# Attention stacks of block 0: two split parts per transfer by way of a buffer in memory, mask rows from memory, clearing moved to GpSimd

## The reference, cut to what matters

```
for i in range(NL):                                       # NL = 6 layers
    ...                                                   # self attention
    q = rope((xn @ cq_w[i].T).reshape(B, L, H, HD))       # 16 sequences x 56 queries
    k = rope((context @ ck_w[i].T).reshape(B, LC, H, HD)) # 16 sequences x 1500 keys
    v = (context @ cv_w[i].T).reshape(B, LC, H, HD)       # H = 16 heads of HD = 8 features
    scores = einsum('bqhd,bkhd->bhqk', q, k) / sqrt(HD)
    scores = where(mask, -inf, scores)
    x = x + einsum('bhqk,bkhd->bqhd', softmax(scores), v).reshape(B, L, D) @ co_w[i].T
    ...                                                   # MLP
```

## Time and profile before

| | us |
|---|---|
| median of 3 runs | 7625.0 |
| the profiled execution's own time | 7628.34 |
| its span, first to last instruction | 7626.5 |
| first and last query transfer issued in block 0 | 236.2 and 4312.5 |
| mean granted TensorE clock, share of full | 0.891 |

### The profile page before, as it was taken

How to read it: one execution, slowest core, us unless ns; L and a number is a source line. 1 busy time by engine, 2 the same in 40 slices (tenths; PEclk the granted TensorE clock), 3 DMA queues, 4 the chain that set the end, 5 groups by cost and what they waited for, 6 DMA issues and landing times.

```text
span 7626.5 us, 148949 instructions
## 1 busy us (share of the span) xinstructions
PE 6404.8 (84%) x58485; PEld 4540.6 (60%) x58485; DVE 4073.1 (53%) x8998; ACT 3384.9 (44%) x6385; POOL 2280.8 (30%) x2182
## 2 busy tenths in 40 slices
PE   5587877878787887878786788999987999999998
PEld 3365555546465555546464436777764777774883
DVE  2465666656565666656565452444444444445562
ACT  1355554555454554545454432344432333332573
POOL 4344444434443444434443200000000111107440
PEclk6698988989898888889888897999987999999997
DMA  1455445555555545554454301000000000003000
GB/s 42 70 78 79 80 78 84 76 82 79 81 77 80 81 78 82 79 83 77 81 78 78 51 29 22 33 33 29 29 20 20 13 13 13 13 9 101 1 1 20
DMA packets 405818, 410.92 MB, mean 54 GB/s; under 512 B 134791, under 2 KB 382162, under 8 KB 403074
## 3 DMA queue, kind: packets, MB, share of 16 engines
q1 hardware_dynamic: 405122, 401.39, 30.6%
HBM read 158.00 MB, written 0.46 MB: 21 GB/s over the span
## 4 chain that ended last, share of the span: by engine, by line
PE 43%; SPq 33%; issue 7%; POOL 5%; DVE 4%; ACT 4%; DMA 3%; POOLq 1%; DVEq 0%; ACTq 0%
SPq L1443 17%; PE psum L2251 9%; PE psum L2218 8%; SPq L1452 8%; SPq L1464 7%; PE psum L2263 3%; PE psum L1587 3%; PE psum L1532 3%; POOL slot_context L3407 2%; DMA query_stack<-query_parts 2%; PE psum L437 2%; PE psum L1565 2%; PE psum L423 2%; PE psum L1552 2%; POOL key_parts L2078 1%
## 5 line engine op out<-in xcount | busy, mean ns | idle before, releaser
L1928 DVE TENSOR_REDUCE row_max<-psum 128x1 f32<-128x500 f32 x2304 | 1449.2, 670 | 842.0 <-PE psum L1552 838.2
L2048 ACT ACTIVATE weights<-psum 125x448 f32<-125x448 f32 x2304 | 1230.6, 543 | 1452.3 <-PE psum L1532 1439.9
L1532 PEld LDWEIGHTS psum<-query_stack,key_stack 128*125 128x125 bf16 x9216 | 795.1, 146 | 624.3 <-issue 453.2
L1532 PE MATMUL psum<-query_stack,key_stack 128*125 128x112 bf16 x9216 | 1031.4, 238 | 121.6 <-ACT weights L2048 121.1
L1552 PE MATMUL psum<-key_stack,query_stack 64*64 64x500 bf16 x4608 | 502.5, 425 | 676.9 <-DMA query_stack<-query_parts 527.3
L2775 POOL TENSOR_TENSOR l_ctx_v<-l_ctx_v,l_ctx_w 125x512 f32<-125x512 f32 x48 | 61.0, 1271 | 2286.1 <-DVE l_ctx_v L2769 2286.1
L2251 PE MATMUL psum<-l_ctx_v,l_turned 125*128 125x128 f32 x5376 | 713.6, 281 | 16.4 <-ACT l_turned L2289 12.4
L1565 PE MATMUL psum<-weights,values 125*17 125x112 f32 x18432 | 719.9, 278 | 0.7 <-issue 0.5
L2331 DVE TENSOR_REDUCE l_stat<-psum 128x1 f32<-128x1500 f32 (+1 forms) x224 | 391.6, 1748 | 574.3 <-PE psum L2218 574.3
L2251 PEld LDWEIGHTS psum<-l_ctx_v,l_turned 125*128 125x128 f32 x5376 | 643.1, 191 | 59.2 <-ACT l_turned L2289 40.2
L2075 POOL TENSOR_TENSOR key_temp<-key_temp,key_parts 128x500 f32<-128x500 f32 x288 | 327.2, 1136 | 1054.8 <-ACT key_parts L1954 1054.8
(11 more groups left out here) (531 smaller groups left out, 10514.9 us busy)
## 6 DMA issues: line engine op xcount, KB each, us to landing
key_stack<-key_parts SPq DMA_DIRECT2D x3456, 62.5 KB
ctx_t<-in_ctxT SPq DMA_DIRECT2D x96, 750.0 KB
l_ctx_v<-in_ctxV SPq DMA_DIRECT2D x32, 750.0 KB
key_stack<-ctx_mask_rows SPq DMA_DIRECT2D x1152, 3.9 KB
query_stack<-query_parts SPq DMA_DIRECT2D x1152, 14.0 KB
l_ctx_t<-in_ctxT SPq DMA_DIRECT2D x16, 750.0 KB
slot_context<-in_ctxV SPq DMA_DIRECT2D x16, 750.0 KB
sm_w<-in_sm_w SPq DMA_DIRECT2D x3, 2048.0 KB
```

The source lines that it names most:

```text
L1532: mm = e.matmul(self.k.psum[0:KN, h, (p % 4) * QC:(p % 4 + 1) * QC], ks[:, p, kt * KN:(kt + 1) * KN], q[:, p * QC:(p + 1) * QC])
L1928: e.tensor_reduce(self.largest[:, TWOS * h + p // 2, c:c + 1], k.psum[:, 2 + h, 0:500], AX.X, ALU.max, negate=True).then_inc(self.max_read ...
L2048: e.activation(half(self.p[kt % 2], h), self.k.psum[0:KN, h, 0:HALF], ACT.Exp).then_inc(self.exped.sem, 1)
```

## The change

All of it is in block 0, save for three semaphores that are now shared with a late block under new names.

- A chunk of keys is first written from `key_parts` to a DRAM buffer in one DMA (`write_keys`, [128, 3, 500], four buffers). SP waits for it to land, then issues 6 DMAs from DRAM into the stack instead of 12 from SBUF. Each carries two parts of 64 features, that is 16 partitions and 128 pieces of 1000 bytes. Its source is [2 parts, 64 features, 500 columns], with the part first. In one of three the same part is read twice, with a step of 0.
- Part order in the stack changes from keys 0,0,1,1,0,2 with queries 0,1,0,1,2,0 to keys 0,1,0,0,1,2 with queries 0,1,1,2,0,0: the same six products.
- Queries likewise: one write to DRAM, a wait, 6 DMAs of 16 partitions.
- The mask is written to DRAM once; per slot 2 DMAs of 8 pieces of 3000 bytes replace 12.
- `key_parts` and `query_parts` are free again when the write has landed, not when the stack is filled.
- SP's order in a slot becomes: stack chunk 0 with masks, write chunk 1, weights, write and stack queries, stack chunk 1, write chunk 2, fetch, stack chunk 2, write the next slot's chunk 0.
- The clearing in the loop goes from DVE to POOL at the same step, with a drain before, between and after its two copies.

```diff
-K_PARTS, Q_PARTS = (0, 0, 1, 1, 0, 2), (0, 1, 0, 1, 2, 0)
-PART_ROW = (0, 8, 16, 24, 48, 56)
+K_PARTS, Q_PARTS = ((0, 1), (0, 0), (1, 1)), ((0, 1), (1, 1), (0, 0))
+PART_ROW = (0, 16, 48)
...
+def two_parts(a, h, first, step):
+    v = a[64 * h:64 * h + 64, first:first + 1 + step, :]
+    return (v if step else v.broadcast_to([64, 2, a.shape[2]])).rearrange("q i c -> i q c")
...
+        self.k_memory = k.nc.dram_tensor("key_parts_memory", (4, 128, 3, 500), BF16).ap()
+        self.mask_memory = k.nc.dram_tensor("ctx_mask_memory", (B, L), BF16).ap()
+        self.q_memory = k.nc.dram_tensor("query_parts_memory", (128, 3, QC), BF16).ap()
...
+    def write_keys(self, e, s, c):
+        n = 3 * s + c
+        e.wait_ge(self.key_lo.sem, self.key_lo(s, c))
+        e.dma_start(self.k_memory[n % 4], self.k_part[n % 2][:, :, :]).then_inc(self.part_written[n % 2].sem, 16)
+
     def stack_keys(self, e, s, c):
-        part, sem = self.k_part[n % 2], self.part_stacked[n % 2].sem
+        part, sem = self.k_memory[n % 4], self.part_stacked[n % 2].sem
-        e.wait_ge(self.key_lo.sem, self.key_lo(s, c))
+        e.wait_ge(self.part_written[n % 2].sem, self.part_written[n % 2](n // 2))
+        if n >= 2:
+            e.wait_ge(sem, self.part_stacked[n % 2](n // 2 - 1))
-        for i, j in enumerate(K_PARTS):
+        for row, two in zip(PART_ROW, K_PARTS):
             for h in range(2):
-                row = 64 * h + PART_ROW[i]
-                e.dma_start(dst[row:row + F1, :, c * 500:(c + 1) * 500], part[64 * h:64 * h + 64, j, :]).then_inc(sem, 16)
+                lo = 64 * h + row
+                e.dma_start(dst[lo:lo + 2 * F1, :, c * 500:(c + 1) * 500], two_parts(part, h, *two)).then_inc(sem, 16)
...
-            for n in range(6):
-                for row in (32, 96):
-                    e.dma_start(dst[row:row + 1, :, n * 250:(n + 1) * 250],
+            for row in (32, 96):
+                e.dma_start(dst[row:row + 1, :, :], self.mask_memory[b:b + 1, :].unsqueeze(1).broadcast_to(
+                    [1, PAIRS, L])).then_inc(self.mask_stacked.sem, 16)
+
+    def write_queries(self, e, s):
+        e.wait_ge(self.q_lo.sem, self.q_lo(s))
+        if s >= 1:
+            e.wait_ge(self.q_stacked[(s - 1) % 3].sem, self.q_stacked[(s - 1) % 3]((s - 1) // 3))
+        e.dma_start(self.q_memory, self.q_part[:, :, :]).then_inc(self.q_written.sem, 16)
...
@@ def gpsimd
+                if kt == 7 and 3 <= s + 2 < NS:
+                    e.drain()
+                    self.clear(e, s + 2)
+                    e.drain()
                 self.key_gpsimd(e, s, kt)
```

More of the change, by code:

```diff
@@ L1295, in __init__ @@
         self.ctx_arrived = [ev(f"ctx_t{i}_arrived", NS // 2, step=16) for i in range(2)]
-        self.part_stacked = [ev(f"key_part{i}_stacked", NS * 3 // 2, step=32 * len(K_PARTS)) for i in range(2)]
-        self.mask_stacked = ev("key_mask_stacked", NS, step=192)
-        self.q_stacked = [ev(f"query_stack{i}_arrived", NS // 3, step=32 * len(Q_PARTS)) for i in range(3)]
+        self.part_stacked = [ev(f"key_part{i}_stacked", NS * 3 // 2, step=32 * len(PART_ROW)) for i in range(2)]
+        self.mask_stacked = ev("key_mask_stacked", NS, step=32, base=16)
+        self.q_stacked = [ev(f"query_stack{i}_arrived", NS // 3, step=32 * len(PART_ROW)) for i in range(3)]
         self.key_turned = ev("l0_key_turned", NS, 3)
@@ L1317, in __init__ @@
         self.cleared = ev("l0_max_cleared", NS)
+        self.part_written = [ev(n, NS * 3 // 2, step=16) for n in ("key_part0_written_or_slot_w", "key_part1_written_or_consts")]
+        self.q_written = ev("query_parts_written_or_sigma", NS, step=16)
+        self.k_memory = k.nc.dram_tensor("key_parts_memory", (4, 128, 3, 500), BF16).ap()
+        self.mask_memory = k.nc.dram_tensor("ctx_mask_memory", (B, L), BF16).ap()
+        self.q_memory = k.nc.dram_tensor("query_parts_memory", (128, 3, QC), BF16).ap()
         self.scored = ev("l0_scored", NS, KT, 2)
@@ L1446, in stack_keys @@
                 e.wait_ge(self.masks_ready.sem, self.masks_ready())
+                e.dma_start(self.mask_memory.rearrange("b (n c) -> (b n) c", n=6), self.mask_rows).then_inc(
+                    self.mask_stacked.sem, 16)
+                e.wait_ge(self.mask_stacked.sem, self.mask_stacked(0) - 32)
             else:
@@ L1449, in stack_keys @@
             b = s % B
-            for n in range(6):
-                for row in (32, 96):
-                    e.dma_start(dst[row:row + 1, :, n * 250:(n + 1) * 250],
-                                self.mask_rows[6 * b + n:6 * b + n + 1, :].unsqueeze(1).broadcast_to(
-                                    [1, PAIRS, 250])).then_inc(self.mask_stacked.sem, 16)
+            for row in (32, 96):
[6 more added lines that the diff above has]
+        e.dma_start(self.q_memory, self.q_part[:, :, :]).then_inc(self.q_written.sem, 16)
     def stack_queries(self, e, s):
         dst, sem = self.q_stack[s % 3], self.q_stacked[s % 3].sem
-        e.wait_ge(self.q_lo.sem, self.q_lo(s))
+        e.wait_ge(self.q_written.sem, self.q_written(s))
         if s >= 3:
             e.wait_ge(self.scored.sem, self.scored(s - 3, KT - 1, 1))
-        for i, part in enumerate(Q_PARTS):
+        for row, two in zip(PART_ROW, Q_PARTS):
             for h in range(2):
-                row = 64 * h + PART_ROW[i]
-                e.dma_start(dst[row:row + F1, 0:QW].rearrange("j (p c) -> j p c", p=PAIRS),
-                            self.q_part[64 * h:64 * h + 64, part, :]).then_inc(sem, 16)
+                lo = 64 * h + row
+                e.dma_start(dst[lo:lo + 2 * F1, 0:QW].rearrange("j (p c) -> j p c", p=PAIRS),
+                            two_parts(self.q_memory, h, *two)).then_inc(sem, 16)
     def fetch(self, e, s):
@@ L1500, in sync @@
             if 0 <= s + 2 < NS:
+                if s + 2 == 0:
+                    self.write_keys(e, 0, 0)
                 self.stack_keys(e, s + 2, 0)
-            if 0 <= s + 2 < NS:
-                self.stack_keys(e, s + 2, 1)
+                self.write_keys(e, s + 2, 1)
             if s >= 0 and b == 7 and l + 1 < NL:
@@ L1517, in sync @@
             if 0 <= s + 2 < NS:
+                self.write_queries(e, s + 2)
                 self.stack_queries(e, s + 2)
-                self.stack_keys(e, s + 2, 2)
+                self.stack_keys(e, s + 2, 1)
+                self.write_keys(e, s + 2, 2)
             if 2 <= s + 4 < NS:
                 self.fetch(e, s + 4)
+            if 0 <= s + 2 < NS:
+                self.stack_keys(e, s + 2, 2)
+            if 1 <= s + 3 < NS:
+                self.write_keys(e, s + 3, 0)
     def score_tensor(self, e, s, kt, h):
@@ L1803, in others, with clear @@
             "r (g c x) -> r g c x", g=TWOS, c=2)[:, :, :, h * S:(h + 1) * S]
-    def clear_vector(self, e, b):
+    def clear(self, e, b):
         if b >= 3:
@@ L1809, in clear_vector @@
         for h in range(2):
+            if h == 1:
+                e.drain()
             op = e.tensor_copy(self.others(b, h, 16), self.no_max[64 * h + 32:64 * h + 48, :].unsqueeze(2).unsqueeze(
@@ L1909, in vector @@
         for b in range(3):
-            self.clear_vector(e, b)
+            self.clear(e, b)
         e.drain().then_inc(self.ones_ready.sem, 1)
@@ L1930, in vector @@
                 self.fixed_vector(e, s, kt)
-                if kt == 7 and 3 <= s + 2 < NS:
-                    self.clear_vector(e, s + 2)
         e.wait_ge(self.side.emptied("down", 2 * NL), self.side.after("down", 2 * NL))
@@ L1962, in fixed_scalar @@
             if b > 0:
[L1963 removed]
+                e.wait_ge(self.q_written.sem, self.q_written(b - 1))
             e.activation(self.q_part[:, 0, :], self.q_tmp[:, 0, :], ACT.Copy).then_inc(self.q_hi.sem, 1)
@@ L2975, in __init__ @@
         self.z1, self.around, self.z2 = (spent[:, i * G:(i + 1) * G] for i in range(3))
-        self.raw_arrived = sig("slot_w_arrived", step=48)
+        self.raw_arrived = sig("key_part0_written_or_slot_w", step=48)
         self.ctx_arrived = [sig(f"ctx_{'tv'[i // 2]}{i % 2}_arrived", 4, step=16) for i in range(4)]
         self.ctx_ready = sig("ctx_normed", B)
-        self.made = sig("consts_ready")
-        self.sigma_ready = sig("slot_sigma_ready")
+        self.made = sig("key_part1_written_or_consts")
+        self.sigma_ready = sig("query_parts_written_or_sigma")
         self.folded = sig("heads_folded", 2)
```

3 lines of the change are left out of this document (1 added, 2 removed).

## The result

The changed kernel takes 10,040.85 us (median of 4 runs, 10,038.11 to 10,043.6) against 7630.98 (now 4 runs): a ratio of 1.3163, with a 95% interval of 1.3138 to 1.3189. The forecast was 10,330, the range 8800 to 12,300.

What follows compares the result with a forecast made beforehand. SP's issuing was nearly full, with key transfers a second limit. After the change two engines carry 63.4 us of work plus 7.5 of waits, 70.9 a slot for 42.8; over 96 slots 2698, plus 5, on 7628: 10,330 us, range 8800 to 12,300.

Steps and rivals of the forecast that it cites:

- Engine count: Block 0 stack transfers: the source leads with 2 parts, so they run on 2 engines, the same 2 each time.
- Price of a key piece: Block 0 key stack transfers: 45 ns for each 1000-byte piece from memory, 51.8 us a slot on the two engines.
- Queries: Block 0 query stack transfers: 384 pieces of 224 bytes at 17 ns, 6.5 us a slot.
- Waits for the added writes: SP in block 0 waits for its writes to land while the two engines run dry: 7.5 us a slot.
- the rest: Other block 0 work on the two engines: fetch 1.8 us, key writes 2.8, query write and masks 0.5 a slot.
- A miss without effect: SP's own writes in block 0 were to land 15 us and more after issue, queued behind six transfers.
- Clearing at nothing: Clearing moved from DVE to POOL in block 0 costs nothing; without cover, 2.3 us a slot, 220 us.
- Computation never starves the queue: Block 0 computation needs 37 us a slot and goes on during transfers, so the order never starves the queue.
- The share and the rate: Sign in block 0: DMA share about 0.2 at about 63 GB/s, PE busy below 60%, low granted clock more often.
- A: Rival for block 0 stack transfers: the 16 target partitions decide, 16 engines share the work, 6950 us; chance 0.11.
- C: Rival for block 0: A's engines, but the write, wait, stack round trips take the gain back, about 7625 us; chance 0.01.
- B: Rival for block 0 key transfers: two engines, but 119 ns a piece as in the backlog, 18,700 us; chance 0.08.

## Why the prediction was right

The growth is 25.1 us a slot where 28.1 was forecast, and it comes by the mechanism forecast: the two engines that carry the stack transfers set the slot. The sizes of the terms were off by −2.8 us (keys), −1.1 (queries) and about +0.9 (the waits, by subtraction), so the total is close without large errors having cancelled. By the steps:

- **Engine count.** 2 engines from the smaller leading count: shares of 0.14, 0.27, 0.55 and 1.12 at counts of 2, 4, 8 and 16, and 10,041, 7708 and 7266 us at 2, 4 and 16 (SP's issues differ too, 31, 55 and 43 a slot: the slowest has the fewest, but between 4 and 16 they may carry a part). The Trainium skill's rule for the number of engines (DMA: Bandwidth & Descriptors, Why a DMA increments its semaphore by 16 and not by 1) agrees with each of these shares; the trace of before had shown it only for other shapes.
- **Price of a key piece.** 45 ns was taken, 42.5 is what the backlog window gives and 43.4 what leaving out a third gives. Keys cost 18 x 64 x 42.5 = 49.0 us, not 51.8.
- **Queries.** 17 ns taken; 32 GB/s over two engines are 14 ns, 5.4 us for 6.5.
- **Waits for the added writes.** 7.5 us forecast. Slot less work, 67.9 − (49.0 + 5.4 + 5.1 for the rest as forecast), leaves 8.4. The trace gives a second measure: over one slot (2004.5 to 2072.5, in windows of 0.5 us) the DMA share falls short of the 0.135 of two full engines by 6.4 us in all, 3.5 of them with no traffic, after the writes of queries and of chunk 0 in full and of chunk 2 in part, as forecast. The other 2 us are not accounted for; they may lie in the rest, whose 5.1 nothing measured. Removing only these waits was not tried.
- **A miss without effect.** The writes were to land 15 us and more after issue, behind six transfers. The median is 9.1 us, the longest 11.1. SP doesn't get six transfers into the queue: its issues stretch to 2.7 us each, so by my reading only about three stand ahead of the write.
- **Clearing at nothing.** Held, in two settings.
- **Computation never starves the queue.** From 300 to 6500 us SP waits 1732 us for its own writes to land and less than 10 for computation, and PE's long waits on DMAs are all on transfers into the stacks, as said.
- **The share and the rate** in block 0 came out at 0.22 and 68 GB/s for 0.2 and 63; PE busy 57% for under 60%, at a granted clock of 0.73 for 0.87.
- **Two slips without effect.** The rows of SP's slot add up to 41.3 us, not 39.8, so SP was nearer to full than said. The bounds of the waits are three times 1 and 3.5 us, where the forecast of 7.5 counts two and a half waits; with 2.5 the range would shift by some 50 us at the low end and 170 at the high end.

Of the rivals, A (16 engines) is nearest to the run with the leading count of 16, which has 12 issues a slot more. It was put at 6950, and the measured 7266 is 316 us, 3.3 us a slot, above. A had PE's waits for transfers at nothing, and 2.3 us a slot are still there. A also took 45 ns a piece, where the bursts of 16 engines on 16 rows give 107 to 125 ns (9.3 to 8.0 GB/s an engine); that this makes the waits is likely and not isolated from the added issues. With 32 rows and fewer issues the time comes to 7092. C, that the round trips take the gain of 16 engines back, fails by the same runs: 7266 and 7092 with all three round trips are below 7625. B's price of 119 ns is real for 8 engines on 8 rows (105 from memory) and does not hold for 2 engines on 16 rows, which B had assumed.

## What to carry to other kernels

Count the transfers and then the engines of each: in this kernel half the transfers with twice the bytes lost 2410 us on 2 engines and won 372 on 16 (7266 against 7638 for the kernel before, measured beside it). When a source has to be regrouped, put the order into the memory buffer, so that the long count leads; here one layout was worth 2775 us. A DMA share of 0.14 in the backlog while PE waited for transfers was the sign of it.

## What the runs showed of the hardware that I had not expected

- One engine moves 1000-byte pieces from memory into the stack at 23.3 to 23.5 GB/s when 2 or 4 work on 16 rows, at 9.5 when 8 write 8 neighbouring rows, at 15.4 when 8 write 16 rows (one window of one run), and at 8.0 to 9.3 when 16 write 16 rows.
- SP's issue of a transfer stretches from 0.6 to 2.7 us once about three transfers of 64 pieces an engine are queued. That is the time in which two engines move one such transfer, so I read it as the queue's time and not SP's.
- A transfer that runs on 2 engines costs SP no more to issue than one on 8 (0.61 to 0.63 us for the first ones of a key group, 0.61 before).
